# A convolution block and a windowed attention block: the second norm's weight and bias moved into the first MLP layer, and that layer's matmul split into high and low parts

## The reference

```
y   = layernorm(x) * norm1_w + norm1_b, rolled by (-3, -3), cut into 7x7 windows
qkv = win @ qkv_w.T ; 8 heads of 16 ; softmax(q k / 4 + position bias + mask) v
x   = x + (out @ proj_w.T + proj_b), rolled back
z   = layernorm(x) * norm2_w + norm2_b
out = x + gelu(z @ fc1_w.T + fc1_b) @ fc2_w.T + fc2_b        (exact gelu, 128 -> 512 -> 128)
```

## Time and profile before

| | us |
|---|---|
| median of 3 runs | 5296.85 (5293.0 to 5299.09) |
| the profiled execution's own time | 5297.13 |
| its span, first to last instruction | 5295.3 |
| TensorE busy | 4843.6 (91%) |
| VectorE busy | 3643.9 (69%) |
| ScalarE busy | 3405.9 (64%) |
| GpSimd busy | 2623.6 (50%) |

### The profile page before, as it was taken

The page is one execution under the profiler, slowest core; times in us unless marked ns, Lnnn a source line. Parts: engine busy times, 40 slices in busy tenths (PEclk is TensorE's granted clock), DMA queues, the critical chain, the costliest instruction groups (busy, mean ns, idle before and its releaser), DMA issues.

```text
span 5295.3 us, 197343 instructions
## 1 busy us (share of the span) xinstructions
PE 4843.6 (91%) x73224; PEld 3669.2 (69%) x73224; DVE 3643.9 (69%) x7453; ACT 3405.9 (64%) x5387; POOL 2623.6 (50%) x3763
## 2 busy tenths in 40 slices
PE   3688888599999999999999999999999999999998
PEld 1455566477777777777777777777777777777776
DVE  2233333577777777777777777777777777777775
ACT  1233333377777777777777777777777777777776
POOL 6233333355555555555555555555555555555554
PEclk7899999799999999999999999999999999999999
DMA  2344443100000000000000000000000000000000
GB/s 63 103 130 129 133 130 117 34 26 25 26 26 26 26 26 26 26 25 25 26 26 25 25 26 26 26 26 25 25 25 26 26 26 26 26 26 26 26 25 22
DMA packets 304837, 219.26 MB, mean 41 GB/s; under 512 B 49206, under 2 KB 252008, under 8 KB 304680
## 3 DMA queue, kind: packets, MB, share of 16 engines
q1 hardware_dynamic: 304680, 216.83, 14.0%
HBM read 111.15 MB, written 111.94 MB: 42 GB/s over the span
## 4 chain that ended last, share of the span: by engine, by line
PE 70%; DVE 15%; issue 8%; ACT 3%; SPq 2%; DVEq 1%; POOL 1%; DMA 0%; ACTq 0%; POOLq 0%
PE bank L659 13%; PE bank L651 11%; PE bank L575 9%; DVE xn L1012 8%; PE bank L582 7%; PE bank L592 5%; PE bank L517 5%; PE bank L638 4%; PE bank L567 4%; DVE sc L987 4%; PE bank L530 4%; ACT shared L823 2%; PE bank L605 2%; PE bank L628 2%; PE bank L617 2%
## 5 line engine op out<-in xcount | busy, mean ns | idle before, releaser
L659 PE MATMUL bank<-fc_sb,g 128*98 128x128 f32 x8192 | 998.6, 275 | 1.5 <-ACT g L817 1.5
L659 PEld LDWEIGHTS bank<-fc_sb,g 128*98 128x98 f32 x8192 | 910.2, 165 | 19.8 <-ACT g L817 2.7
L651 PE MATMUL bank<-zt,fc_sb 128*128 128x392 f32 x2048 | 895.0, 519 | 3.0 <-ACT zt L810 2.3
L1153 POOL TENSOR_TENSOR res<-x,projb 98x512 f32<-98x512 f32 x256 | 325.4, 1271 | 1122.2 <-DVE x L1029 1122.2
L1012 DVE TENSOR_SCALAR xn<-x,lnp 98x128 f32<-98x128 f32 x1024 | 838.1, 879 | 4.0 <-POOL lnp L1082 4.0
L1171 POOL TENSOR_TENSOR sc<-sc,mx 128x784 f32<-128x784 f32 x512 | 775.5, 1517 | 11.2 <-DVE mx L993 3.3
L987 DVE TENSOR_TENSOR sc<-bank,shared 128x392 f32<-128x392 f32 x1024 | 528.8, 558 | 324.5 <-PE bank L592 324.4
L817 ACT ACTIVATE g<-bank,fc1b 128x392 f32<-128x392 f32 x1024 | 586.7, 587 | 247.8 <-PE bank L651 244.5
L605 PEld LDWEIGHTS bank<-ident_sb,sc 128*98 128x98 f32 x4096 | 465.2, 127 | 174.7 <-issue 98.1
L1082 POOL TENSOR_TENSOR lnp<-st 98x8 f32<-98x8 f32 x777 | 144.9, 214 | 847.9 <-DVE st L875 847.9
L971 DVE TENSOR_TENSOR shared<-bank,vmask_sb 98x512 f32<-98x512 f32 x512 | 354.0, 691 | 283.0 <-PE bank L575 283.0
(11 more groups left out here) (87 smaller groups left out, 7698.9 us busy)
## 6 DMA issues: line engine op xcount, KB each, us to landing
x<-x_scratch SPq DMA_DIRECT2D x768, 49.0 KB
out_x<-y SPq DMA_DIRECT2D x672, 49.0 KB
xc_even<-in_x SPq DMA_DIRECT2D x128, 196.0 KB
shared<-in_x SPq DMA_DIRECT2D x128, 196.0 KB
x_scratch<-xc_even SPq DMA_DIRECT2D x128, 196.0 KB
x_scratch<-shared SPq DMA_DIRECT2D x128, 196.0 KB
x<-x_scratch SPq DMA_DIRECT2D x256, 38.5 KB
out_x<-y SPq DMA_DIRECT2D x224, 38.5 KB
```

Source lines behind the costliest of these rows:

```text
L651: nc.tensor.matmul(ring[:, 0:ST], fc1[:, 128 * j:128 * j + 128], zt[:], start=True, stop=True).then_inc(full, 1)
L659: mm = nc.tensor.matmul(RC[0:PT, C * p:C * p + C], g[:, c, PT * p:PT * p + PT], fc2[:, c, :], start=c == 0, stop=c == HC - 1)
```

## The change

The second norm's weight and bias go into the first MLP layer. In the preparation, fc1 is multiplied by norm2_w, row by row, and fc1b gets fc1's product with norm2_b, by four matmuls of one column. ScalarE's eviction of the transposed z is a plain copy. And the hidden matmul isn't float32 any more: the scaled fc1 is split once into `fc1_hi`, a tile of type fp32r (a float32 that TensorE takes in reduced precision), and `fc1_lo`, what is left; zt is split in each strip into `zt_hi` (ScalarE's copy) and `zt_lo` (PSUM minus zt_hi, on VectorE, a new operation between the two value evictions). `hidden` then issues three matmuls that accumulate: hi by hi, lo by hi, hi by lo. Its first one waits for both parts.

```diff
 BIAS_PREP = [..., "hidden_ps", "hidden", "table_ps", "table",
+             "fc1b_ps", "fc1b", "fc1_scaled", "fc1_hi", "fc1_lo"]
...
+        fc1_hi, fc1_lo = [sb(f"fc1_{i}", [C, HID], fp32r) for i in ("hi", "lo")]
-        zt = sb("zt", [C, ST])
+        zt_hi, zt_lo = [sb(f"zt_{i}", [C, ST], fp32r) for i in ("hi", "lo")]
...
+                    at(pe, "fc1b_ps")
+                    pe.wait_ge(wload, 16 * len(LOADS))
+                    for j in range(HC):
+                        mm = nc.tensor.matmul(bank[2][:, j:j + 1], fc1[:, 128 * j:128 * j + 128], ln[:, 3:4],
+                                              start=True, stop=True)
+                    mm.then_inc(prep, 1)
...
             def hidden(t, j):
                 pe.wait_ge(c_out, C_JOBS * t.n + 1 + j // 2)
+                if j == 0:
+                    pe.wait_ge(zt_split, t.n + 1)
...
-                nc.tensor.matmul(ring[:, 0:ST], fc1[:, 128 * j:128 * j + 128], zt[:],
-                                 start=True, stop=True).then_inc(full, 1)
+                cols = slice(128 * j, 128 * j + 128)
+                nc.tensor.matmul(ring[:, 0:ST], fc1_hi[:, cols], zt_hi[:], start=True, stop=False)
+                nc.tensor.matmul(ring[:, 0:ST], fc1_lo[:, cols], zt_hi[:], start=False, stop=False)
+                nc.tensor.matmul(ring[:, 0:ST], fc1_hi[:, cols], zt_lo[:], start=False, stop=True).then_inc(full, 1)
...
             def zt_out(t):
                 act.wait_ge(c_full, C_JOBS * t.n + 1)
-                nc.scalar.activation(zt[:], RC[:, 0:ST], ACT.Identity, scale=ln[:, 2:3],
-                                     bias=ln[:, 3:4]).then_inc(c_out, 1)
+                nc.scalar.activation(zt_hi[:], RC[:, 0:ST], ACT.Copy).then_inc(c_out, 1)
...
                     dve.wait_ge(wload, 16 * len(LOADS))
+                    step("fc1b", V.tensor_tensor, out=fc1b[:], in0=bank[2][:, 0:HC], in1=fc1b[:], op=ALU.add)
+                    step("fc1_scaled", V.tensor_scalar, fc1[:], fc1[:], ln[:, 2:3], None, ALU.mult)
+                    step("fc1_hi", V.tensor_copy, fc1_hi[:], fc1[:])
+                    step("fc1_lo", V.tensor_tensor, out=fc1_lo[:], in0=fc1[:], in1=fc1_hi[:].bitcast(fp32),
+                         op=ALU.subtract)
...
+            def zt_rest(t):
+                dve.wait_ge(c_out, C_JOBS * t.n + 1)
+                V.tensor_tensor(out=zt_lo[:], in0=RC[:, 0:ST], in1=zt_hi[:].bitcast(fp32),
+                                op=ALU.subtract).then_inc(zt_split, 1)
...
                 if t.there():
                     v_out(t, 0)
+                if t3.there():
+                    zt_rest(t3)
                 if t.there():
                     v_out(t, 1)
```

More of the change, by code:

```diff
@@ L138 @@
 BIAS_PREP = ["abs", "exp", "ln", "positive", "softplus", "denominator", "sigmoid", "recip", "product", "magnitude",
-             "sign", "scaled", "exponent", "power", "signed", "tab", "hidden_ps", "hidden", "table_ps", "table"]
+             "sign", "scaled", "exponent", "power", "signed", "tab", "hidden_ps", "hidden", "table_ps", "table",
+             "fc1b_ps", "fc1b", "fc1_scaled", "fc1_hi", "fc1_lo"]
 PREP = CONV_PREP + BIAS_PREP
@@ L251, in program @@
         xc_biased, xc_summed, xc_relu = sem("xc_biased"), sem("xc_summed"), sem("xc_relu")
+        zt_split = sem("zt_split")
         conv2_begun = sem("conv2_begun")
```

## The result

| | us |
|---|---|
| before, median of 4 executions | 5297.02 (5293.0 to 5299.09) |
| after, median of 4 executions | 5265.62 (5261.68 to 5272.07) |
| ratio | 0.9944, 95% interval 0.9929 to 0.996 |
| the profiled execution of after: own time, span | 5272.07, 5270.2 |

31 us were gained where 12 were forecast. The mechanism was the forecast's. Of the terms of its sum the ring's gain was too small, the head's 4 us did not reach the end, and the tail cost 3 us instead of 1.

A forecast was written before the change was run, and what follows sets the result against it. A ring through GpSimd sets every other strip and would then set all, though TensorE is 96% busy. 5297.1 - 17.5 (ring) + 4 (head) + 1 (tail) gives 5285 us; range 5235 to 5345, its own 5274 to 5294.

The forecast's parts named there:

- the ring: Per strip: value matmuls' end, eviction, statistics, GpSimd's factors, subtractions, residual, last xn, transposes, back; 16.75 and 16.52 us, without hidden matmuls.
- the ring's gain: In the steady strips: 16.66 to 16.59 us, 0.07 a strip, 17.5 us over 250 strips; bounds 10 to 25.
- the head: Before the first convolution, once: four one-column matmuls and four VectorE steps add 4 us, covered by nothing.
- the tail: Last three strips, only the MLP left: copy, VectorE's part and first hidden matmul add 0.3 us each, 1 us together.
- turn: Start of TensorE's transposes of xn in each strip; forecast 16.5 to 16.7 us apart, each waiting for VectorE.
- the relief: TensorE's saving in the four hidden matmuls: 0.165 us each, 0.66 us a strip, nine tenths going into waiting.
- One clock a column: Each fp32r matmul streams 392 columns in 0.163 us, loads hidden; three take 0.49 us against 0.66 for f32.
- the prediction's own formula: TensorE's time per strip with a hidden matmul of h us: 16.58 + 4 x (h - 0.66).
- the rival with two bare loads: Two of three fp32r weight loads not hidden: hidden matmul 0.71 us, total 5332; chance 0.06 for all bare-load cases.
- The two-clock rival: fp32r takes two clocks a column: hidden matmul 0.98 us, TensorE 17.89 a strip, total 5610 us; chance 0.14.
- TensorE's order: TensorE's own sequence of work in a strip: 16.58 us before, forecast to fall to 15.92.
- VectorE at nothing: The new VectorE subtraction, 0.56 us between the value evictions, costs no time, with 0.38 us to spare.

The follow-up runs named there:

- e1: Changed kernel with only the hi by hi hidden matmul, the other two left out: 5263.79 us, ratio 0.9941 to the kernel before.
- e2: Changed kernel with GpSimd's MLP residual moved from behind the subtractions to the head of its turn: 5159.33 us, ratio 0.9746 to the kernel before.
- e3: Kernel before, without the change, with GpSimd's MLP residual moved ahead of the subtractions: 5275.94 us, ratio 0.9964.
- e9: Changed kernel with GpSimd's residual early and only the hi by hi hidden matmul: 5022.41 us, ratio 0.9484 to the kernel before.
- e4: Changed kernel with VectorE's subtraction for zt_lo done twice, once into a spare tile: 5359.59 us, ratio 1.0123 to the kernel before.
- e7: Changed kernel with one extra VectorE statistics operation right ahead of xn: 5301.42 us, ratio 1.0015 to the kernel before.
- e12: Changed kernel with GpSimd's residual early and VectorE's zt_lo subtraction done twice: 5282.60 us, ratio 0.9978 to the kernel before.
- e5: Kernel before with only fc1 scaled, fc1b corrected and the plain ScalarE copy; one f32 hidden matmul, no split: 5295.06 us, ratio 1.0.

## Why the prediction was right, and where its terms were off

**The ring: right.** "None of the four hidden matmuls lies on this ring", "TensorE then waits 0.6 to 0.7 us at each turn": all turns wait for xn, 0.42 and 0.57 us in turn by the weight loads, less than I had put as the relief was less. e1, e2, e3 and e9 show the rule from four sides. Without it, 0.45 us a strip of relief would have read as about 5184 (5297.0 less 250 strips of it).

**One clock a column: right for the streaming, wrong for the loads.** The second and third matmul start 0.17 to 0.18 us apart, 392 columns at one 2.4 GHz clock each being 0.163. But the first to the second is 0.26 to 0.28. The weight loads in order:

```profile
3010.97 0.19 PEld L663 LDWEIGHTS bank<-zt_hi,fc_hi 128*128 128x128 f32 x1
3011.08 0.19 PEld L664 LDWEIGHTS bank<-zt_hi,fc_lo 128*128 128x128 f32 x1
3011.26 0.19 PEld L665 LDWEIGHTS bank<-zt_lo,fc_hi 128*128 128x128 f32 x1
```

The second load begins 0.11 after the first, takes 0.19, and its matmul starts when it ends, at 3011.26. An f32 instruction streams for 0.33 us, longer than a load; at 0.163 it is shorter. I had set 0.11, the distance of two loads, against 0.163, where the load's own 0.19 counts too. Not all of the 0.26 is the second load's: the first matmul's record starts 0.03 behind its own load, that of an f32 one 0.11 (3007.01 and 3006.90), so I read a part of it as the first load; the records do not divide it. A hidden part is 0.62 to 0.73 us to the next instruction against 0.66 to 0.85, and TensorE's relief 0.45 us a strip, not 0.66. By the prediction's own formula that is a hidden matmul of 0.55 us, between its 0.49 and the 0.71 of the rival with two bare loads. This step was wrong and cost nothing, as TensorE was not the limit.

The two-clock rival fell by this trace. The figure that I had taken for it from the Trainium skill, SBUF — State Buffer, "A bandwidth-pool intuition that's wrong", is one for bf16; as a limit for 4-byte operands it does not hold here, with 392 columns in 0.175 us. The Trainium skill, FP8 and Floating Point Precision, TensorE Precision Notes, names four passes for true FP32 and, for reduced precision, a read of the 4-byte value that is then truncated. That this is a single pass was my inference, and the trace agrees with it: 0.175 us against 0.66 for the whole f32 matmul.

**The ring's gain: 0.07 us a strip forecast, 0.12 found,** 29 us instead of 17.5, and above the bounds of 0.04 to 0.10. As forecast, TensorE's order (16.58) no longer holds the strip whose ring is shorter (16.52). The rest is GpSimd's distance from first subtraction to residual: 3.06 and 2.99 us before, 2.92 after, where I had left 2.99 standing. Two things make it up.

The first is the wait for the second maximum, which I had read as 0.08 us in one strip of two. It was there in both. The maximum on VectorE and the second subtraction on GpSimd, in the faster strip of the kernel before:

```profile
3029.61 0.97 DVE L993 TENSOR_REDUCE mx<-sc 128x16 f32<-128x784 f32 x1
...
3030.66 1.53 POOL L1171 TENSOR_TENSOR sc<-sc,mx 128x784 f32<-128x784 f32 x1
```

And after:

```profile
3016.68 0.97 DVE L1015 TENSOR_REDUCE mx<-sc 128x16 f32<-128x784 f32 x1
...
3017.93 1.50 POOL L1195 TENSOR_TENSOR sc<-sc,mx 128x784 f32<-128x784 f32 x1
```

Before, the subtraction starts 0.08 us after the maximum ends in every strip, the same 0.08 as in e4, where its wait stands in the bracket. After, it starts 0.19 to 0.28 behind and waits no more: it follows the first subtraction by 1.46 us, where it was 1.56 and 1.49. So the waits were 0.10 and 0.03. The smaller one has no bracket, as the records of two subtractions in a row overlap by 0.04.

The second is the subtraction's own length, 1.53 before and 1.50 after. It goes with xn's first operation. Where that asked 0.16 or 0.17 us ahead of the second subtraction it got in at once (0.33 or 0.34 us: before, e4, e7's one strip), ended 0.17 us into it, and the subtraction took 1.52 to 1.54. Where it had asked 0.28 us or more ahead and was held (0.41 to 0.49: after), it ended 0.12 into it, and the subtraction took 1.50. e7 tells the two apart: in its faster strip xn's first operation gets in at once, and the second subtraction starts 1.46 after the first but lasts 1.53. The 1.46 belongs to the maximum, the 1.50 to the request. e7 also shows that the moment of the request matters, with 0.15 us a strip. Why the subtraction is shorter behind a held request no run shows.

**VectorE at nothing: right for the time.** 0.38 us of cover were left ahead of the second value eviction, as worked out. The tight side is the other one, the signal to TensorE, for which I had 0.07 us to spare and 0.06 to spend. Nothing was to spare. The first hidden weight load starts 0.12 us after zt_lo ends (3010.86 to 3010.97), and so it does in e4, where it openly waits (3014.61 to 3014.72). It stands 0.80 behind the start of the value matmuls, where that of the fourth part stands 0.76 behind the transposes ahead of it; so I read 0.04 us of waiting in every strip, a part of what is missing from TensorE's relief. It has no price at the turn, but a second ring runs behind it (e4, e12). "a delay up to 0.17 us only eats the matmul's saving" named the consumer without its ring.

**The head: +4 forecast, 3.8 measured at its place, nothing at the end.** The memset that stood at 115.41 stands at 119.23. "Nothing covers it" failed: in the stretch from 180 to 200 us no engine is busy for more than 3.5 of the 20 us in either kernel, and the DMAs are at half share. From the table by stretches, kernel before:

```profile
180.00:200.00 20.00, 1.81 (x24) 1.54 (x40) 0.78 (x2) 0.00 (x0) 0.17 (x1) 0.50 0.50 151
```

The core waits there for a DMA of the input. TensorE's first work behind it, before and after:

```profile
198.19 1.56 PE L488 MATMUL bank<-ident_sb,xc_even 98*128 98x98 f32 x8 [35.26 <-DMA xc_even<-in_x]
```

```profile
196.47 1.57 PE L497 MATMUL bank<-ident_sb,xc_even 98*128 98x98 f32 x8 [28.65 <-DMA xc_even<-in_x]
```

A delay of 3.8 us goes into a wait of 35, and the next 3x3 convolution starts at 199.68 before and 197.97 after. The first turn falls anywhere from 970.0 to 978.6 us over the twelve profiled kernels, with no order by the preparation; e5's ratio of 1.0 says the same.

**The tail: +1 forecast, +3.0 measured** from the last turn to the end. In the three strips with no other work ScalarE's copy and VectorE's difference stand one behind the other:

```profile
5242.01 0.42 PE L663 MATMUL bank<-zt_hi,fc_hi 128*128 128x392 f32 x1 [1.72 <-DVE zt_lo L995]
```

It starts 2.25 us after the transposes before it (5239.76), where the kernel before took 1.30 (5266.47 to 5267.77): 0.95 more, and 0.96 and 0.50 in the strips on either side, where I had counted 0.46. Two of the three also ran into a slower clock. In the kernel before, TensorE's clock was granted at 1.00 until 5287.6. After, it fell to 0.50, the lower level, from 5228.1 to 5231.5 and from 5252.0 to 5255.4, in the midst of hidden matmuls and shortly behind waits of 1.72 and 1.28 us for zt_lo. The second of these stretches in the table (length, TensorE's matmuls and loads, VectorE, ScalarE, GpSimd, granted clock, DMA share, GB/s):

```profile
5252.00:5255.20 3.20, 3.20 (x10) 2.77 (x10) 0.00 (x0) 1.18 (x2) 0.00 (x0) 0.50 0.18 47
```

At this clock an fp32r matmul takes 0.33 us from start to start instead of 0.175, so these ten cost about 1.5 us more (an estimate from the two distances). e3, which has nothing of the change, shows one such fall in its tail too (5259.0 to 5262.4). How the 3 us divide between the later start and the clock, and whether the change brought the clock's share, is not shown.

**In sum,** between the two profiled executions (spans 5295.3 and 5270.2, 25.1 less): first turn 0.8 later, 28.9 less from first to last turn, 3.0 more behind it. The medians lie 31 apart, and each kernel's executions spread over 6 to 10 us.

## What to carry to other kernels

When an engine is 96% busy, still look whether another ring of engines has the same length, by laying one full turn of it end to end; a relief that is not on the ring turns into a wait. Moving a 1.3 us operation out of the ring was worth 106 us in the changed kernel, more than the change itself, and only 19 us in the kernel before, where TensorE's own order stood right behind: neither of the two shows its worth without the other. Measure a change a second time with the ring loosened before it is judged: 31 us became 117. An empty bracket is not a proof that nothing waited: a distance that stays at its shortest (0.08 us from maximum to subtraction, 0.12 from zt_lo to the weight load) showed two waits that no bracket did. And where a step gets shorter, set what it used to cover (a weight load's full length) against the new length.

## What the hardware showed that I had not expected

An fp32r matmul of 128x392 takes 0.175 us from start to start at a granted clock of 1.00, when its weights are in, against 0.33 for one of the two instructions of an f32 matmul: three of them in 0.62 us at best. At a granted clock of 0.50 it takes 0.33 us. VectorE's 98x128 scale and shift from SBUF to SBUF, 0.34 us alone, ran for 1.67 us when asked for 0.08 us ahead of a GpSimd subtraction and got in at once at 0.17 us ahead: less than 0.1 us in the moment of one engine's request moved the end of the last xn, and the turn with it, by a quarter of a microsecond.
